# Moving one small product group behind a gather, and adding unread products at the end of two attentions

## Time and profile before

| | |
|---|---|
| runs | 671.46, 669.1, 671.15 us |
| profiled execution | 669.4 us, span 667.7 us |
| TensorE busy | 633.4 us, 95% of the span |
| VectorE, ScalarE, GpSimd busy | 63%, 47%, 17% |
| mean granted TensorE clock | 0.991 |

### The profile page before, as it was taken

How to read it: one execution, slowest core, us unless ns; L and a number is a source line. 1 busy time by engine, 2 the same in 40 slices (tenths; PEclk the granted TensorE clock), 3 DMA queues, 4 the chain that set the end, 5 groups by cost and what they waited for, 6 DMA issues and landing times.

```text
span 667.7 us, 14854 instructions
## 1 busy us (share of the span) xinstructions
PE 633.4 (95%) x5897; PEld 553.8 (83%) x5897; DVE 418.9 (63%) x1108; ACT 316.3 (47%) x731; POOL 114.0 (17%) x108
## 2 busy tenths in 40 slices
PE   6999989999989999999999999999999998999997
PEld 6789877566968778988899988899999867889996
DVE  2746583454379457886645546786766748567776
ACT  0256402332221346886357524555545368457663
POOL 1200000022020314440120000264444020000000
PEclk9999999999999999999899989999999999999999
DMA  9960001475500001110000100312222001012000
GB/s 260 386 201 3 3 0 64 172 283 211 148 1 1 0 1 50 48 50 2 1 2 2 50 2 14 100 60 72 66 83 82 25 1 33 28 62 81 26 25 27
DMA packets 16643, 45.54 MB, mean 68 GB/s; under 512 B 3580, under 2 KB 4572, under 8 KB 14847
## 3 DMA queue, kind: packets, MB, share of 16 engines
q1 hardware_dynamic: 13704, 37.75, 17.7%
q0 software_dynamic: 896, 5.77, 2.4%
q10 hardware_dynamic: 1976, 1.08, 0.7%
HBM read 44.12 MB, written 0.44 MB: 67 GB/s over the span
## 4 chain that ended last, share of the span: by engine, by line
PE 76%; DVE 12%; ACT 7%; issue 4%; DMA 1%; POOL 1%; POOLq 0%; DVEq 0%; SPq 0%; ACTq 0%
PE PS L1004 6%; PE PS L1062 6%; PE PS L929 6%; PE PS L938 4%; PE PS L825 3%; PE PS L1025 3%; PE PS L787 2%; PE PS L857 2%; PE PS L684 2%; PE PS L1052 2%; PE PS L1165 2%; PE PS L688 2%; PE PS L686 2%; PE PS L687 2%; PE PS L685 2%
## 5 line engine op out<-in xcount | busy, mean ns | idle before, releaser
L2311 POOL TENSOR_TENSOR rstd<-var,nhalf 96x3 f32<-96x3 f32 x18 | 17.3, 961 | 287.9 <-DVE var L1601 287.9
L684 PE MATMUL PS<-XH,WH 128*128 128x288 f32 x156 | 48.0, 308 | 3.3 <-DVE OT L1870 1.4
L1322 ACT ACTIVATE MIX<-PS 128x288 f32<-128x288 f32 x54 | 22.2, 411 | 51.6 <-PE PS L688 51.4
L686 PE MATMUL PS<-XH,WL 128*128 128x288 f32 x156 | 46.0, 295 | 0.0
L685 PE MATMUL PS<-XL,WH 128*128 128x288 f32 x156 | 46.0, 295 | 0.0
L687 PE MATMUL PS<-X,WH 128*128 128x288 f32 x156 | 46.0, 295 | 0.0
L688 PE MATMUL PS<-X,WL 128*128 128x288 f32 x156 | 45.9, 294 | 0.0
L1453 ACT ACTIVATE VS<-PS 128x384 f32<-128x384 f32 x48 | 23.1, 486 | 32.1 <-PE PS L1004 25.1
L736 PE MATMUL PS<-AH,DW 128*128 128x288 f32 x102 | 32.2, 316 | 4.4 <-DVE AL L1881 4.3
L929 PE MATMUL PS<-wqkv_l1f,XT 128*96 128x256 f32 (+1 forms) x144 | 34.3, 387 | 0.9 <-ACT XT L1213 0.9
L2349 POOL TENSOR_TENSOR ssq<-ssq,nhalf 96x12 f32<-96x12 f32 x12 | 27.2, 2267 | 46.3 <-DVE ssq L2135 46.3
(11 more groups left out here) (317 smaller groups left out, 1796.5 us busy)
## 6 DMA issues: line engine op xcount, KB each, us to landing
RG<-in_gu_l0f_dram SPq DMA_DIRECT2D x4, 1024.0 KB, 8.7
GU<-in_gu_l0f_dram SPq DMA_DIRECT2D x4, 1024.0 KB, 11.9
RG<-in_gu_l2f_dram SPq DMA_DIRECT2D x9, 384.0 KB, 3.5
RG<-in_gu_l2f_dram SPq DMA_DIRECT2D x18, 192.0 KB, 4.2
RD<-in_wd_l2f_dram SPq DMA_DIRECT2D x9, 288.0 KB, 2.9
RD<-in_wd_l3f_dram SPq DMA_DIRECT2D x6, 384.0 KB, 3.0
BIG<-in_patch_dram SPq DMA_DIRECT2D x6, 288.0 KB, 7.4
RD<-in_wd_l0f_dram SPq DMA_DIRECT2D x4, 384.0 KB, 8.4
```

The lines of the kernel that those rows point to most:

```text
L684: mm(o, WH[r][:, 0, w], XH[:, cols], start=True, stop=False)
L686: mm(o, WL[r][:, 0, w], XH[:, cols], start=False, stop=False)
```

## The change

`positions()` and ScalarE's copy of its result move behind the third block of the sort. Behind the turn at the end of A1 seven unread products are added, and four at the end of A2; both write bank 3.

```diff
                 for i in range(T0 + 2):
                     if i == LATE:
                         gather(RANKS - 1)
+                        positions()
                     if i < T0:
                         up(i)
-                    if i == 0:
-                        positions()
...
                 pe.wait_ge(S["s_taken"], u0 + a.units)
                 turn(stage + 1, 0)
+                if wide:
+                    keep_clock(7 if a is A1 else 4, 3, CT)
                 pe.wait_ge(S["o_sb"], u0 + a.units)
                 output(range(TAU, NG), range(a.ng - 2, a.ng)).then_inc(S["y_ready"], 1)
...
                 for i in range(T0 + 2):
                     if i == LATE:
                         sorted_rows(RANKS - 1)
+                        act.wait_ge(S["m0_post"], 1)
+                        activation(POST.rearrange("p (j n) -> p j n", j=2), PS[:, 6:8, 0:HN], ACT.Copy).then_inc(S["m0_post_sb"], 1)
                     if i < T0:
                         silu(i)
-                    if i == 0:
-                        act.wait_ge(S["m0_post"], 1)
-                        activation(POST.rearrange("p (j n) -> p j n", j=2), PS[:, 6:8, 0:HN], ACT.Copy).then_inc(S["m0_post_sb"], 1)
```

## The result

The changed kernel takes 667.77 us in the median of 16 executions (664.94 to 671.63); the kernel before took 671.96 us in the median of 16 (665.88 to 679.5). The ratio is 0.9945 with a 95% interval of 0.9925 to 0.9966: by the ratio 3.7 us faster (the two medians lie 4.2 us apart), where 0.2 us was forecast.

The account below looks back on a forecast made before the run. TensorE's own work was taken as the bound, 76% of the span, so time moves only where it idles or gets more work. -1.3 + 0.6 + 0.5 = -0.2 us from 671.15 gives about 671.0 us, range 668.6 to 672.6.

Parts of the forecast that it names:

- The places, -1.3: In the sort, spreading the places behind the third block's gather fills TensorE's 1.27 us idle: -1.3 us.
- the cover: In the sort, the places' spread on TensorE fits inside the wait for ScalarE's two copies, from about 115.4 to 116.8.
- the rival of the unkept gain: In the sort, late weight loads for blocks 4 to 11 cancel the gain: sum +1.1, 672.3 us; chance 0.12.
- A1's seven products, +0.6: Behind A1's turn, seven products take 0.92 us with no wait to fill; later slack leaves +0.6 us.
- A2's four, +0.5: Behind A2's turn, four products take 0.53 us with no idle to fill, delaying what follows: +0.5 us.
- the chain named: After A1's turn, later outputs delay VectorE's addition of half 1 by 0.82 us, then statistics, root and normalising.
- The sum, -0.2: Whole kernel: -1.3 + 0.6 + 0.5 = -0.2 us, applied to the median for about 671.0 us.
- The clock, taken as unchanged: Whole kernel: executions differ by where clock drops of about 1.45 us fall; the sum is applied to the median.
- The rival of the spared drop: Behind the turn, on A2's split products or M2, added products prevent a fourth drop: -1.45, about 669.5 us; chance 0.18.

Follow-up runs that it names:

- the true waits: Places moved, no products behind the turns; 7 and 3 unread products in the waits ahead of A1's and A2's output products instead: 665.5 and 665.69 us.
- weak filler: Changed kernel with its 7 and 4 products replaced by 6 and 3 transposing products of 8 columns: 672.62 us, ratio 1.0023.
- the shift put back: Ten unread products added behind the moved places: 672.61 us on the kernel with only the places moved, 669.78 us on the changed kernel.

## Why the prediction was wrong

*The places, -1.3:* right. -1.34 in the trace and -1.4 ±0.1 at full clock over 24 executions; the cover fits "almost to the edge", as said, and no transfer came late (TensorE busy 51.75 of 51.75 us from block 1 on), so the rival of the unkept gain is out.

*A1's seven products, +0.6, and A2's four, +0.5:* right in the trace, +0.59 and +0.51, by the chain named: no wait stood behind the turns, and half 1's addition came late, by 0.81 us at A1. At full clock the changed kernel stands 0.9 ±0.2 us above the places alone.

*The sum, -0.2:* -0.24 in the trace, -0.4 ±0.15 at full clock.

*The clock, taken as unchanged:* this step failed. It is the sentence "I take it that the executions differ by where the drops fall. I apply the sum to the median". It was true that they differ so; it didn't follow that the change leaves the drops alone. The mean lost clock went from 8.2 to 4.9 us, which is worth 2.6 us of the 3.0 between the means; the medians of these samples lie 3.6 us apart. The rival of the spared drop had the right kind of cause, but one drop as its price, 0.18 as its chance, only the added products as what spares it, and a place behind the turns where no trace of before or of the changed kernel has a drop. It was held down by one trace, in which no drop lies behind a turn, and one trace holds one outcome of several.

*What the runs put in its place:* fewer drops, with two causes, of which each is shown in part. That activity moves the clock is shown: in the true waits the same kind of products cost no time and took 2.8 ±1.0 us off the lost clock, and products against a weak filler of nearly the same length made 5.0 ±1.2. How much the products behind the turns spare against nothing is weakly known. It is 1.3 ±0.8 us with the places moved, 0.6 ±0.8 without, and 4.2 ±1.3 between the two kernels with the shift put back. The shift in time is supported, not settled: the places alone spare 1.9 ±0.7 us, filling their wait spares none, and the shift put back undoes it (3.6 ±1.2); but the changed kernel with the shift put back keeps more of its gain than it should. Grouping the kernels by where their later work stands gives the same picture. At the old time the lost clock is 8.2 to 9.9 us without products and 5.6 to 7.6 with both sets; 1.3 us earlier it is 6.2 and 4.9. The weak filler's kernel doesn't fit it: it stands at the earlier time, with no products, at 9.9. How much of the products' share belongs to A1 and how much to A2 stays open; that A2's alone cost 0.9 ±0.25 us at full clock, and 0.51 in the trace, may be noise.

## What to carry to other kernels

Where the granted clock drops in one execution and not in the next, one trace is one draw: take the mean granted clock of every execution beside its time, and compare kernels both at full clock and in lost clock, before a small edit is priced at its steps alone. Put unread products where TensorE truly idles between thin work (the rows with an idle time, not the `wait` in the code): there they cost nothing, while behind a turn whose wait was over they cost most of their time (0.59 of 0.92 us, 0.51 of 0.53), and only spared drops could pay for that. An edit that shifts later work by a microsecond seems able to move a kernel's time by more than its own steps (here 1.4 us of steps and 1.9 ±0.7 us of lost clock), and such a gain needn't survive the next edit.

## What was not expected of the hardware

- In the weak filler's kernel the clock fell to 0.50 at 399.60 after TensorE had been busy 3.40 of 3.40 us with small products and transposes.
- The drops of one kernel recur in place: the first at 299.9, 300.28 and 300.6 us in three executions; two more followed it in the first two and none in the third.
- A microsecond of lost clock costs 0.81 us of time, fitted within the kernels over all executions.
- The 122 executions of the kernel before run from 666.0 to 680.4 us, mostly by their drops (lost clock 2.7 to 19.0 us); the one with products in the true waits 662.7 to 671.6.
